# Four graph layers on one Trainium2 core: order of the first feature-weight products, and a ring of three buffers in the third layer

## What is computed

```
h = relu(layernorm(x)); x += elu([softmax(mask(e)) @ h, -softmax(mask(-e)) @ h] @ wtrans)   # e = leaky_relu(s_i + t_j), s, t = (h @ W) @ a
h = relu(layernorm(x)); x += relu((D^-1/2 adj D^-1/2 @ h) @ W1 + b1)                         # D = row sums
h = relu(layernorm(x)); x += relu(adj @ ((h > 0) @ sign(W2).T))
h = relu(layernorm(x)); s = h @ W3;  x += (1 - t) * s + t * (adj @ s)
```

## Time and profile before

| what | value |
|---|---|
| median of three runs | 964.89 us |
| the profiled execution's own time | 965.67 us |
| its span, first to last instruction | 964.0 us |
| TensorE / VectorE / ScalarE / GpSimd busy | 933.9 / 743.3 / 540.9 / 94.1 us |
| mean granted TensorE clock | 0.988 of full speed |

### The profile page before, as it was taken

One profiled execution on the slowest core, in us unless ns is written; L12 is line 12 of the kernel. 1 busy time (PEld: TensorE's weight loads), 2 busy tenths in 40 slices (PEclk: granted clock), 3 DMA queues, 4 the chain that ended last, 5 costly groups with the idle time before them and its releaser, 6 DMA issues.

```text
span 964.0 us, 18964 instructions
## 1 busy us (share of the span) xinstructions
PE 933.9 (97%) x7105; PEld 689.2 (71%) x7105; DVE 743.3 (77%) x1112; ACT 540.9 (56%) x934; POOL 94.1 (10%) x206
## 2 busy tenths in 40 slices
PE   9889999999999999999999999999999989999995
PEld 8457788888888888888888455555788845555553
DVE  7697899999999999999996776656447755655664
ACT  6476899999999999999985611111223331111010
POOL 4100001000010001000030000000024430000000
PEclk9899999999999999999999999999999999999998
DMA  4915276677576666658312425655247726666642
GB/s 178 96 45 77 23 100 76 66 89 96 48 96 83 81 66 86 86 51 109 46 39 100 173 94 203 211 183 203 114 181 281 276 79 213 215 227 205 201 153 65
DMA packets 39883, 120.80 MB, mean 125 GB/s; under 512 B 4604, under 2 KB 24597, under 8 KB 39701
## 3 DMA queue, kind: packets, MB, share of 16 engines
q1 hardware_dynamic: 27653, 97.94, 29.0%
q0 software_dynamic: 10944, 21.30, 25.5%
q10 hardware_dynamic: 1232, 0.85, 0.3%
HBM read 169.48 MB, written 14.50 MB: 191 GB/s over the span
## 4 chain that ended last, share of the span: by engine, by line
PE 84%; DVE 7%; ACT 3%; issue 2%; POOL 2%; DMA 0%; POOLq 0%; DVEq 0%; ACTq 0%
PE f_ya L1318 23%; PE f_yb L1318 23%; PE f_ya L1495 14%; PE f_ya L1433 12%; DVE f_gb L1856 2%; PE f_ya L1269 2%; PE f_yb L1404 2%; PE f_yb L1376 2%; PE f_yb L1269 1%; PE f_ya L1442 1%; POOL f_gv L960 1%; ACT f_ubuf L1184 1%; ACT f_x_mat L1186 1%; DVE f_stats L1600 1%; PE f_yb L1302 1%
## 5 line engine op out<-in xcount | busy, mean ns | idle before, releaser
L1318 PE MATMUL f_ya<-f_x_mat,f_s_mat 128*128 128x257 f16 x2028 | 334.6, 273 | 1.9 <-DVE f_x_mat L1664 1.9
L1318 PE MATMUL f_yb<-f_x_mat,f_s_mat 128*128 128x257 f16 x2028 | 333.2, 273 | 0.0
L1318 PEld LDWEIGHTS f_yb<-f_x_mat,f_s_mat 128*128 128x128 f16 x2028 | 198.2, 98 | 24.8
L1318 PEld LDWEIGHTS f_ya<-f_x_mat,f_s_mat 128*128 128x128 f16 x2028 | 194.5, 98 | 27.2 <-issue 2.8
L1030 ACT ACTIVATE f_gb<-f_e_tile,f_expc 128x256 f32<-128x256 f32 x338 | 144.5, 494 | 9.3 <-DVE f_s_mat L1694 9.3
L1856 DVE SCALAR_TENSOR_TENSOR f_gb<-f_gb 128x1664 f32<-128x1664 f32 x52 | 97.7, 1886 | 18.0 <-DMA f_gb<-adj_dram 18.0
L1689 DVE SCALAR_TENSOR_TENSOR f_s_mat<-f_wm,f_s_mat 128x1792 f16<-128x1792 f32 (+1 forms) x52 | 98.4, 1892 | 12.1 <-ACT f_s_mat L1041 8.5
L1683 DVE TENSOR_TENSOR f_wm<-f_gb,f_a 128x1792 f32<-128x1792 f32 (+1 forms) x52 | 98.1, 1887 | 3.2 <-issue 1.6
L1684 DVE SCALAR_TENSOR_TENSOR f_gb<-f_gb,f_a 128x1792 f32<-128x1792 f32 (+1 forms) x52 | 98.1, 1887 | 0.0
L1694 DVE SCALAR_TENSOR_TENSOR f_s_mat<-f_gb,f_s_mat 128x1792 f16<-128x1792 f32 (+1 forms) x52 | 98.0, 1886 | 0.0
L1041 ACT ACTIVATE f_s_mat<-f_wm 128x1792 f16<-128x1792 f32 (+1 forms) x52 | 82.5, 1587 | 22.0 <-DVE f_wm L1683 20.9
(11 more groups left out here) (185 smaller groups left out, 938.2 us busy)
## 6 DMA issues: line engine op xcount, KB each, us to landing
f_gb<-adj_dram SPq DMA_DIRECT2D x52, 832.0 KB, 5.0
f_a<-f_a_dram SPq DMA_DIRECT2D x23, 832.0 KB, 5.9
f_wm<-f_a_dram SPq DMA_DIRECT2D x16, 832.0 KB, 4.6
f_rows<-adj_dram POOLq DMA_DIRECT2D x24, 416.0 KB, 8.2
f_a<-adj_t_dram POOLq DMA_DIRECT2D x26, 224.0 KB, 4.9
f_a_dram<-f_a SPq DMA_DIRECT2D x26, 224.0 KB, 5.3
f_a<-adj_t_dram POOLq DMA_DIRECT2D x26, 192.0 KB, 6.9
f_a_dram<-f_a SPq DMA_DIRECT2D x26, 192.0 KB, 4.2
```

The lines of the kernel that those rows point to most:

```text
L1318: return pe.matmul(bank[:, 0:F + 1], s_mat[:, j, side, i], x_mat[:, j, x_side, 0:F + 1], start=start, stop=stop)
```

## The change

1. Lead-in. ScalarE's two conversions of `wtrans` stand after `high_turned(9)` and `high_turned(10)`; VectorE's two `weight_low` stand after `low_turned(11)` and `low_turned(12)`. On TensorE `weigh(0, 2)` stands ahead of the wait for the scores and the product of L1291, and `weigh(2, 4)`, which was the beginning of the next `weigh`, stands right behind it, ahead of the wait for `edone`.
2. Third layer, buffers. Pairs 3 to 12 take turns in three buffers (`ring2`): the lower buffer of `wm` and the two of `a8`. Pair q + 3 is loaded when pair q is multiplied. TensorE's loop is written out. The loads of the fourth layer's slots 1, 2 and 3 stand in the order 3, 2, 1.
3. Third layer, VectorE. The order in pair k is update(2k), update(2k + 1), check (pairs 1 to 10), norm(2k), norm(2k + 1).

```diff
+        def ring2():
+            return [(wide[0][:, 0], extra_here[0], 3), (a8[:, 0], pair_here[2, 0], 1), (a8[:, 1], pair_here[2, 1], 2)]
...
                     if q == 1:
                         load_pair(2, 4, 0)
                         load_pair(2, 5, 1)
-                    elif q < 4:
-                        load_slot(q - 2)
-                    elif q < PAIRS - 2:
-                        load_pair(2, q + 2, q % 2)
+                    elif q == 2:
+                        load_slot(0)
+                    elif q < PAIRS - 3 and q % 3 == 0:
+                        load_extra(q + 3, 0)
+                    elif q < PAIRS - 3:
+                        load_pair(2, q + 3, q % 3 - 1)
                     else:
-                        load_slot(q - PAIRS + 4)
+                        load_slot(PAIRS - q)
...
                 for m in range(PAIRS - UP_PAIRS - 1, PAIRS):
                     high_turned(m)
-                a.wait_ge(late_here, 32)
-                for s in range(2):
-                    a.activation(wt16[:, 0, ...], wtrans_sb[...], ACT.Copy, ...).then_inc(wt16_done, 1)
+                    if PAIRS - 5 < m < PAIRS - 2:
+                        s = m - (PAIRS - 4)
+                        if s == 0:
+                            a.wait_ge(late_here, 32)
+                        a.activation(wt16[:, 0, ...], wtrans_sb[...], ACT.Copy, ...).then_inc(wt16_done, 1)
...
+                pe.wait_ge(wt16_done, 4)
+                weigh(0, 2)
                 pe.wait_ge(dotd, 6)
                 pe.matmul(op[:, 0:2 * P], ones[:], w_res[:, 0:2 * P], start=True, stop=True).then_inc(extd, 1)
-                pe.wait_ge(wt16_done, 4)
-                weigh(0, 2)
+                weigh(2, 4)
                 pe.wait_ge(edone, 2)
...
-                                weigh(2, Z_AHEAD[0])
+                                weigh(4, Z_AHEAD[0])
...
-                pair2(3, 1, 16, wide[0][:, 0], extra_here[0])
-                pair2(4, 0, 32, a8[:, 0], pair_here[2, 0])
-                with pe.Fori(0, (PAIRS - 5) // 2) as k:
-                    for i in range(2):
-                        pair2(2 * k + 5 + i, 1 - i, 16 * k + 32 + 16 * i, a8[:, 1 - i], pair_here[2, 1 - i])
+                for q in range(3, PAIRS):
+                    rows, here, loads = ring2()[q % 3]
+                    pair2(q, q % 2, 16 * ((q - loads) // 3 + 1), rows, here)
...
                 for n in range(5, PAIRS):
                     low_turned(n)
-                for s in range(2):
-                    weight_low(s)
+                    if n > PAIRS - 3:
+                        weight_low(n - (PAIRS - 2))
...
                             if layer == 2:
                                 update(t, p, k, r=r)
-                                if not (first and p == 0):
-                                    norm(t - 1, 1 - p)
+                                if p == 1 and 0 < k <= CHECKS1 + 4 - CHECKS2:
+                                    check(CHECKS2 + k - 1, (CHECKS2 + k - 1) % 2)
+                                if p == 1:
+                                    norm(t - 1, 0)
+                                    norm(t, 1)
                                 continue
...
                             pair(q, False, r=q % 2)
-                            if CHECKS2 + q - 1 < CHECKS1 + 4:
-                                check(CHECKS2 + q - 1, (CHECKS2 + q - 1) % 2)
...
-                    if layer == 2:
-                        norm(TILES - 1, 1)
```

More of the change, by code:

```diff
@@ L996, in _ @@
                     high_turned(m)
-                a.wait_ge(late_here, 32)
-                for s in range(2):
-                    a.activation(wt16[:, 0, :, s * F:(s + 1) * F], wtrans_sb[:, s * FB:(s + 1) * FB, :], ACT.Copy,
-                                 scale=WT if s == 0 else -WT).then_inc(wt16_done, 1)
+                    if PAIRS - 5 < m < PAIRS - 2:
+                        s = m - (PAIRS - 4)
+                        if s == 0:
+                            a.wait_ge(late_here, 32)
+                        a.activation(wt16[:, 0, :, s * F:(s + 1) * F], wtrans_sb[:, s * FB:(s + 1) * FB, :], ACT.Copy,
+                                     scale=WT if s == 0 else -WT).then_inc(wt16_done, 1)
                 a.wait_ge(extd, 2)
```

## The result

The changed kernel takes 979.96 us (median of 6 runs, 978.31 to 980.25) against 963.23 us for the kernel before in the same runs (median of 6; its earlier three, 964.89, are among them). The ratio is 1.0168, 95% interval 1.0151 to 1.0185: slower, as forecast. In the later comparisons the kernel before has medians of 964.18 to 964.85, so some 1 us of the difference of 16.7 may be its low median here.

A forecast was written before the change was run, and what follows sets the result against it. In the third layer VectorE's check was the chain's largest part, TensorE setting the pace again in the fourth. Lead-in -3.1 and VectorE's order +16.9 made +13.8 us on 965.67: 979.5, given as 978.5 us, range 971 to 983.

The forecast's parts named there:

- blocked cycle: Third layer, pairs with a check: the check holds GpSimd to its end, 7.67 us a pair; the blocked case has chance 0.83.
- The step that decided: Third layer: VectorE's check, reading two operands from SBUF, was expected to hold GpSimd's L963 until 0.09 us after its end.
- Rival 1: Third layer: GpSimd isn't held by the check, each of 12 pairs takes 6.24 us; 964.4 us in all, chance 0.09.
- Rival 2: Handover to the fourth layer: GpSimd not held by the check, and TensorE's clock stays up; 962.7 us, chance 0.05.
- Costed at nothing: Third layer's buffers: TensorE's 2.2 us of waits for rows go, but none lies on the chain; no gain.
- Rival 3: Third layer: the rows' transfers set the pace and the third buffer frees it; some 959 us, chance 0.03.
- 3.1 us less: Lead-in: if the clock holds, `weigh(4)` starts at 40.3 us instead of 43.39, and all that follows comes 3.1 us earlier.
- The lower bound: Lead-in: if TensorE's clock falls near 33.4 us anyway, the gain is about 1.3 us.
- the better of two cases: Lead-in: the clock holds, 3.1 us gained, taken over the clock falling anyway, about 1.3 us gained.
- The handover: Third to fourth layer: the 4.72 us from the last pair's first update to TensorE's going on stays; change 0.
- The fourth point: Blocked, but the lead-in's clock falls anyway: 980.5 us; a third-layer fall costs only a microsecond at the handover. No separate chance.

The follow-up runs named there:

- `one_operand`: The changed kernel with the third layer's ten checks replaced by a minimum over the same half tile, reading one operand: 962.31 us, ratio 0.9989 against the kernel before.
- `half_check`: The changed kernel with the third layer's ten checks on half their columns, two operands in SBUF as before: 971.66 us, ratio 1.0078 against the kernel before.
- `lead_buffers`: The changed kernel with VectorE's old order in the third layer; lead-in and three buffers stay: 963.02 us, ratio 0.9991 against the kernel before.
- `lead_only`: The kernel before with the lead-in's part of the change alone: 962.45 us, ratio 0.9984 against the kernel before.
- `lagged_two_buffers`: The changed kernel with norms one pair late, and the two buffers and loop of the kernel before: 952.4 us, ratio 0.9868 against the kernel before.
- `lagged_lead_old`: The changed kernel with norms one pair late, three buffers, and the lead-in of the kernel before: 952.98 us, ratio 0.9886 against the kernel before.
- `lagged`: The changed kernel with norms one pair late and four places for statistics, scales and centred tile: 951.76 us, ratio 0.9863 against the kernel before.
- `norms_first`: The changed kernel with the check behind the two norms of its pair: 981.41 us in one execution.

## Why the prediction was right

**Size and sign.** Forecast 978.5, measured 979.96, within 971 to 983. The sum on the profiled execution was +13.8, the trace has +14.4. That the two are so close owes something to luck: the lead-in gained 1.6 us less than forecast, and the last stretch gave back 0.7 that nobody had counted.

**VectorE's order.** Every term of the blocked cycle is in the trace: forecast 7.67, measured 7.66 or 7.67 in pairs 2 to 10; a pair without a check 6.24, measured 6.25 (709.19 to 715.44) for the first and 6.16 (792.05 to 798.21) for the last. The step that decided, that an instruction of 1.89 us holds GpSimd as one of 0.48 us was seen to, was an inference from three rows; `one_operand`, with the row of L1583, shows that it is the second operand in SBUF, and `half_check` that the length counts. Rival 1, unblocked, would have been right for a check with one operand: 962.31, against 964.4 there. It was costed 0.26 us a pair too high, since the norm that held the second L969 would have come later. Rival 2 needed the unblocked cycle as well, and in `one_operand`, which has it, the clock fell at the handover all the same (0.66 over 780 to 785 us).

**Buffers.** Costed at nothing: `lead_buffers` shows no difference from `lead_only`. Rival 3 is excluded by it. Even where TensorE sets the pace (`lagged_two_buffers`), the third buffer's worth can't be told from nothing.

**The lead-in.** The mechanism was right, the size not for this execution. The term was "3.1 us less", taken because TensorE's idle time shrinks; the clock fell at some 32.5 us all the same and the term measured 1.54. With the clock up, `lead_only` shows 3.4. The lower bound was added up wrongly: 3.1 less 1.5 less 0.6 makes 1.0, not 1.3; and the fall cost less than that, since the clock came back at 36 us. The forecast took the better of two cases as the likeliest. By the medians (-1.7 us for `lead_only`, and -1.2 between `lagged_lead_old` and `lagged`) the lower end was the better centre.

**The handover.** The distance from the last update stayed (4.72 and 4.61). The fourth point also said that a clock falling inside the third layer would leave its pace alone; in `norms_first` it fell there (0.76 over 745 to 750 us), and the cycle stayed 7.97. The last 0.68 us, in the fourth layer, wasn't forecast and wasn't traced further.

## What to carry to other kernels

When two engines' instructions are put side by side to hide a wait, look at what each reads: a long two-operand pass of VectorE over SBUF stops GpSimd's smallest instruction until it ends, and if that instruction is in the chain that VectorE waits for next, hiding becomes adding. Where a result goes round three engines and comes back, don't rearrange the waits within the round; keep one more round in flight, so that the consumer is a whole round late. And a buffer added to an engine that isn't on the chain brings nothing; here not even the shortened chain gave it a worth that could be told.

## What the hardware showed that was not expected

GpSimd's small instructions stood until the end of each two-operand VectorE instruction that they met, for VectorE instructions of 0.48, 1.03 and 1.89 us. The two with one operand (L969 and L962) ended 0.07 to 0.09 us after it, at whatever point they had been caught (1.71 and 1.74 us beside the check). How far behind it the end lies depends on the instruction: the power instruction L966, 0.56 us by itself, met a check in `lagged` and ended 0.42 us after it:

```profile
752.69 1.89 DVE L1863 SCALAR_TENSOR_TENSOR f_gb<-f_gb 128x1664 f32<-128x1664 f32 x1 [0.84 <-DMA f_gb<-adj_dram]
752.83 2.17 POOL L966 TENSOR_TENSOR f_gv<-f_gv,f_minus_half 128x1 f32<-128x1 f32 x1
```

An instruction with one operand in SBUF of the same 1.89 us held nothing. Nor did a two-operand one hold everything of GpSimd's: its start of a transfer takes the usual 0.54 us in the middle of one.

```profile
115.02 1.75 DVE L1684 SCALAR_TENSOR_TENSOR f_gb<-f_gb,f_a 128x1536 f32<-128x1536 f32 x1
115.75 0.54 POOL L936 DMA_DIRECT2D f_rows<-adj_dram  x1 [14.56 <-ACT f_rows L1056]
```

(At 22.93 us one took 0.88 beside VectorE's L1625, an instruction with one 128x256 operand; the runs don't say why.)

The other way round nothing of the kind was seen: while the power instruction of 9.27 us ran that had started at 495.83, VectorE's two-operand instructions at 497.74 and 499.81 took 2.10 and 2.03 us, against 2.02 on average.

And the clock: with the same program order in the lead-in it fell at 32.5 us in one execution, with TensorE in dense products since 32.21, and did not fall in another, with dense products since 32.11; the difference is 1.9 us at the start of the third layer (709.19 and 707.33).
